# A gathered first group in every trip, and the PSUM copy behind it, in a four-layer graph network on one core

## Chip, cores and metric

The kernel runs on one core of one Trainium2 chip. The metric is the device time of one execution in microseconds (us), as the median of several runs. Below, PE is TensorE, ACT is ScalarE, DVE is VectorE, POOL is GpSimd and SP is SyncE, which here only issues DMAs.

## What is computed

Four graph networks follow each other on 3125 nodes with 64 features and 53125 edges that are sorted by target node; after each one, x = layernorm(x + network(x)).

```python
# networks 0 and 1: GIN (64-64-64 with batch norm, then 64-256-256-64)
h = x + segment_sum(x[src], dst)
# network 2: three rounds of messages, each with a GRU cell behind it
m = relu(concat(h[src], h[dst], edge_features) @ W1 + b1) @ W2 + b2
agg = segment_sum(m, dst)
# network 3: two attention layers
e = leaky_relu(alpha_s[src] + alpha_d[dst]); w = exp(e - segment_max(e)[dst])
out = segment_sum(w / (segment_sum(w)[dst] + 1e-16) * (x @ W)[src], dst) + b
```

So there are seven passes over all edges: two of GIN (passes 0 and 1), three of messages (2 to 4) and two of attention (5 and 6). Every pass fetches one row of a node table for each edge.

## The kernel before

**Edges, trips and groups.** Partition p holds 416 consecutive edges, so a "column" is 128 edges, one per partition. Eight columns are a group, four groups (j = 0 to 3) a trip, and a pass has 13 trips (0 to 12), 52 groups. DVE walks the columns of a group one after the other (`running`, L1219, and in attention L1322): a column is added to the one before wherever both edges have the same target, so the last edge of a node ends with the node's sum. SP then stores the group (`store_sums`).

**Two ways to fetch a row.** Of the 32 columns of a trip POOL gathers 20 with one indirect DMA each (`gather_group`, L794), into `ringG`, a ring of eight group slots. The other 12 columns are "fetched" by PE: the table is split into three bf16 parts side by side (128 x 192 for each of 25 blocks of 128 nodes), and a one-hot matrix of block by column picks the rows, 25 x 12 matmuls a trip (L1759), accumulated over the 25 blocks in six PSUM banks, two columns a bank. These 12 columns are the `Hot` pattern: `Hot((3, 3, 3, 3))` fetches the last three columns of each group, and the last trip of a pass `Hot((0, 0, 3, 3))`, so 26 are gathered there and 6 fetched. One trip's matmuls are called a unit here.

**A unit on PE** (`fetch_piece`). It has four pieces of 7, 6, 6 and 6 blocks. Piece 0 opens the banks one after the other, each with a matmul of `opener` (so the trace shows six such rows at the start of a unit), and the opening of a bank waits until ACT has copied the unit before out of that bank (semaphore `evicted`). The last piece closes the banks one after the other (`bank_done`). The banks are not doubled. In the message passes PE also multiplies the edge features of one group after each piece (L1780).

**ACT** does three things in one instruction stream, written out in `act_pass`: `evict` copies the banks of a unit to SBUF (L880), `make_lent` builds one-hot tiles from the node numbers (L913, one ACTIVATE of 128 x 1536 a block), and a group's own work: `clip` is the relu of a message group (L922), `weigh` the exponentials and scalings of an attention group. In pass 0 ACT makes three blocks a piece and DVE the others; in pass 1 ACT makes four blocks in piece 0 and three in each other piece; in passes 2 to 4 one a piece, and the rest is read back from DRAM (`feed_piece` on SP); in the attention passes all is read back. `make_lent(k, i + 2, q)` writes over the tiles that unit i + 1 reads, so it waits until PE has used piece q of unit i + 1 (`hot_used`), and for the last piece until all banks of unit i + 1 are closed (`bank_done`).

**The order on ACT in trip i**: the group's own work for j = 0, `make_lent(i + 2, 0)`, the same for j = 1 and j = 2; at j = 3 first `evict(i + 1)` and then `make_lent(i + 2, 3)`. In message passes four banks are copied before the relu of group j = 3 and two behind it.

**DVE** adds the three parts of the fetched columns and puts them into the ring (`take_products`, L1201 and L1210), before the first group of the trip that has fetched columns: before j = 0, in the last trip before j = 2. POOL gathers a group eight places ahead once its slot is stored, and once the group seven places back is summed.

**SP** issues in program order: reloads of tiles, the node numbers of the fetched columns (`load_sources`), features, stores. Ahead of an attention pass it stores the node table (`tab`) and two values a node (`adtab`) in seven chunks; POOL waits for all of `adtab`, gathers one row of it, and starts the pass.

Of the kernel before, what the change touches and what calls it, by code (L numbers as in the profile page):

```python
# [18 lines left out]
COLS, GROUPS = 8, 4  # L19
# [5 lines left out]
TRIPS = L // SPAN  # L25
# [147 lines left out]
class Pass:  # L173
# [24 lines left out]
    def by_vector(self, q):  # L198
# [3 lines left out]

TILES = [range(0, 7), range(7, 13), range(13, 19), range(19, NT)]
UMAX = 12
HOT, LAST = Hot((3, 3, 3, 3)), Hot((0, 0, 3, 3))
MIXED = 64 + 3 * EF
KEPT = 3
KEEPING = 2
SOURCED = 5
STEP, TOP, PEAK = 4194304.0, 1024.0, 32.0  # L210
PASSES = ([Pass(0, HOT, LAST), Pass(1, HOT, LAST)] + [Pass(2 + l, HOT, LAST) for l in range(NLAYER)]
          + [Pass(5 + l, HOT, LAST, WG) for l in range(2)])
# [12 lines left out]
EIGHTH = L * EF // 8  # L225
COUNT_FROM, COUNT_TRIPS = 4, 6
WEIGHT_TRIPS = 8
EARLY_BANKS = 4
FIRST_AT = 9


# [35 lines left out]
def build(nc, a, out):  # L267
    with ExitStack() as ctx:  # L268
# [153 lines left out]
        def fed_tiles(way, q):  # L422

            size = UMAX * P
            return eighths(way.fed(q).start * size, len(way.fed(q)) * size).bitcast(I16)
# [159 lines left out]
        def _(sp):  # L585
# [56 lines left out]
            def trip(k, i, l=None, after_first=None):  # L642
                if k < SOURCED:
                    if i == 0 and k:
                        load_sources(k, 2)
                for j in range(GROUPS):
                    g = i * GROUPS + j
                    if k < SOURCED and i + 3 < TRIPS and j == (l is not None):
                        load_sources(k, i + 3)
                    if l is not None:  # L650
                        if g + ERING < NG:
                            load_edges(l, g + ERING)
                        if g + QRING - 1 < NG and g:
                            load_starts(l, g + QRING - 1)
                    if k and i + 2 < TRIPS:
                        feed_piece(k, i + 2, j)
                        if l is not None and j == GROUPS - 1:
                            load_hot_edges(l, i + 2)
                    store_sums(k, g)
                    if after_first is not None and j == 0:  # L660
                        after_first()

            def feed_piece(k, i, q):

                way, m = PASSES[k], k * TRIPS + i
                if i == 0:
                    sp.wait_ge(bank_done, BANKS_BEFORE[k])
                elif q < len(TILES) - 1:
                    sp.wait_ge(hot_used, (len(TILES) - 1) * (m - 1) + q + 1)
                else:  # L670
                    sp.wait_ge(bank_done, BANKS_BEFORE[k] + i * way.banks)
                sp.dma_start(fed_tiles(way, q), kept[q][i * P:(i + 1) * P, (way.fed(q).start - TILES[q].start) * UMAX * P // 2:
                                                                 (way.fed(q).stop - TILES[q].start) * UMAX * P // 2]
                             ).then_inc(hot_fed[q], 16)
# [88 lines left out]
            for l in range(2):  # L763
                if l:
                    feed_unit(5 + l, 0)
                for c in range(NC):
                    sp.wait_ge(*done(f"gh{l}", c))
                    sp.dma_start(chunk_of(tab[5 + l], c), chunk(gN, c, WG)).then_inc(table_out, 16)
                    sp.dma_start(chunk_of(adtab[l], c), chunk(adN, c, 2)).then_inc(adtab_out, 16)
                    if l == 0 and c == NC - 4:  # L770
                        sp.wait_ge(*FILL("agg2", NC - 1))
                        feed_piece(5, 0, 0)
                    if l == 0 and c == NC - 2:
                        sp.wait_ge(*FILL("l2_back", NC - 1))
                        for q in range(1, len(TILES)):
                            feed_piece(5, 0, q)
                sp.wait_ge(ad_scattered, 16 * NT * (l + 1))
                sp.dma_start(ad_e[:].rearrange("p l o -> p (l o)"), ad_g).then_inc(ad_in, 16)
                feed_unit(5 + l, 1)
                for i in range(TRIPS):  # L780
                    trip(5 + l, i)
# [83 lines left out]
        def _(act):  # L865
            def evict(k, i, banks=None):

                way, m, unit = PASSES[k], k * TRIPS + i, PASSES[k].unit(i)
                banks = range(unit.banks) if banks is None else banks
                if m and banks.start == 0:  # L870
                    act.wait_ge(parts_used, m)
                if i == 0 and 2 <= k < 5 and banks.start == 0:
                    act.wait_ge(q_scattered, 16 * NT * (k - 1))
                    act.wait_ge(qtable_out, 16 * NC * (k - 1))
                    act.wait_ge(table_out, 16 * NC * k)
                size = 3 * way.fetched
                for b in banks:
                    n = min(2, unit.u - 2 * b)
                    act.wait_ge(bank_done, BANKS_BEFORE[k] + i * way.banks + b + 1)
                    nc.scalar.copy(parts_of(way)[:, 2 * b:2 * b + n].rearrange("p u k d -> p u (k d)"),  # L880
                                   ps[:, b, 0:2 * size].rearrange("p (u x) -> p u x", u=2)[:, 0:n]
                                   ).then_inc(evicted, 1)
# [9 lines left out]
            def make_lent(k, i, q):  # L892

                way, m = PASSES[k], k * TRIPS + i
                if k < KEEPING and (i or q):
                    keep_piece(k, i - (q == 0), (q - 1) % len(TILES))
                if q == 0:
                    act.wait_ge(src_hot_in[m % 2], 16 * (m // 2 + 1))
                if k < KEEPING and i:
                    act.wait_ge(hot_kept[q], 16 * (k * TRIPS + i))  # L900
                if i == 0:
                    if q == 0 and k == 0:
                        act.wait_ge(numbered, 1)
                    elif q == 0:
                        act.wait_ge(bank_done, BANKS_BEFORE[k])
                        if k >= 2:
                            act.wait_ge(*done(f"pq{k - 2}", NC - 1))
                elif q < len(TILES) - 1:
                    act.wait_ge(hot_used, (len(TILES) - 1) * (m - 1) + q + 1)
                else:  # L910
                    act.wait_ge(bank_done, BANKS_BEFORE[k] + i * way.banks)
                for t in way.by_scalar(q):
                    ins = nc.scalar.activation(needed(way, hot_of(way)[t]), needed(way, src_hot[m % 2]),  # L913
                                               ACT.Abs_reciprocal_sqrt, bias=node_minus[:, t:t + 1], scale=STEP, saturate=False)
                ins.then_inc(lent_ready, 1)
# [18 lines left out]
                                         ).then_inc(weighted, 1)  # L934

            def act_pass(k):
                lent, banks = k < SOURCED, PASSES[k].banks
                if lent:
                    for q in range(len(TILES)):
                        make_lent(k, 0, q)  # L940
                    for q in range(len(TILES) - 1):
                        make_lent(k, 1, q)
                evict(k, 0)
                if lent:
                    make_lent(k, 1, len(TILES) - 1)
                for i in range(TRIPS):
                    for j in range(GROUPS):
                        g = i * GROUPS + j
                        if k == 0:
                            zero_starts(g)  # L950
                        elif 2 <= k < 5:
                            if j == GROUPS - 1 and i + 1 < TRIPS - bool(PASSES[k].last.first):
                                evict(k, i + 1, range(EARLY_BANKS))
                            clip(k - 2, g)
                        elif k >= 5:
                            weigh(k - 5, g)
                        if PASSES[k].last.first and i >= TRIPS - 2:
                            if i == TRIPS - 1 and j == PASSES[k].last.first - 1:
                                evict(k, i)
                        elif j == GROUPS - 1 and i + 1 < TRIPS:  # L960
                            evict(k, i + 1, range(EARLY_BANKS if 2 <= k < 5 else 0, banks))
                        if lent and i + 2 < TRIPS:
                            make_lent(k, i + 2, j)
                if k < KEEPING:
                    keep_piece(k, TRIPS - 1, len(TILES) - 1)
# [966 lines left out]
```

## Time and profile before

| | |
|---|---|
| runs, median (lowest, highest) | 3032.32 us (3028.57, 3034.46) |
| profiled execution, its own time | 3030.97 us |
| its span, first to last instruction | 3029.1 us |
| PE busy | 2631.4 us (87%) |
| POOL busy | 2187.9 us (72%) |
| DVE busy | 1936.0 us (64%) |
| ACT busy | 1495.0 us (49%) |
| mean granted TensorE clock | 0.911 of full speed |

The profile is of one execution. A row of a timeline gives start and length of equal neighbouring instructions in us, engine, line, operation, what is written and read, shape, count, and in brackets the idle time of the engine before them with what ended it. A busy PE is modelled from its starts. The granted clock is the share of full speed that PE was given; its two levels are 2.4 GHz (1.00) and 1.2 GHz (0.50). POOL's pause of 0.30 us between two gathers stands as "issue" and is part of a gather's price.

### The profile page before, as it was taken

What the parts mean: (1) busy time and instruction counts of PE and PEld (TensorE: products, weight loads), DVE (VectorE), ACT (ScalarE), POOL (GpSimd) and SP (SyncE); (2) the same over time, 40 slices, a digit from 0 to 9 for tenths busy, and PEclk for the clock granted to TensorE, in tenths of its full rate; (3) what the DMA queues carried; (4) which work ended last, traced back from release to release, by engine and by line L of the source; (5) the groups of instructions that cost most, each with busy time, mean ns of one, the idle gap of its engine ahead of it and who ended that gap; (6) DMA issues with size and microseconds to landing.
All of it is one profiled execution on the core that took longest, in us unless ns stands there. A gap on an engine that the chain in (4) does not pass through costs nothing. (4 is left out here: it accounts for less than half of the span.)

```text
span 3029.1 us, 73919 instructions
## 1 busy us (share of the span) xinstructions
PE 2631.4 (87%) x28348; PEld 2440.9 (81%) x28348; DVE 1936.0 (64%) x6197; ACT 1495.0 (49%) x2632; POOL 2187.9 (72%) x2178
## 2 busy tenths in 40 slices
PE   7999669999699999489997599994899995799981
PEld 7999649999469999279997299994499994699981
DVE  5877743554348888468888568886445555455555
ACT  7877438888234444244443344441634443344443
POOL 6777737777657777677777677776567776777774
PEclk9999859999799999699998799997799997799995
DMA  5666728998348998269997289994287775487761
GB/s 175 219 215 218 202 67 285 359 364 301 118 138 291 302 304 289 82 205 304 305 304 241 86 279 304 303 305 145 39 249 257 257 255 179 110 260 254 260 220 43
DMA packets 321465, 688.68 MB, mean 227 GB/s; under 512 B 114939, under 2 KB 150245, under 8 KB 302708
## 3 DMA queue, kind: packets, MB, share of 16 engines
q1 hardware_dynamic: 227584, 537.99, 52.8%
q0 software_dynamic: 69344, 70.04, 10.2%
q10 hardware_dynamic: 24340, 78.40, 6.6%
q8 instruction: 78, 1.28, 0.2%
q14 instruction: 119, 0.97, 0.1%
HBM read 487.50 MB, written 198.70 MB: 227 GB/s over the span
## 5 line engine op out<-in xcount | busy, mean ns | idle before, releaser
L1759 PE MATMUL ps<-big 128*128 128x192 bf16 (+1 forms) x25275 | 2260.8, 248 | 1.8 <-issue 1.7
L1759 PEld LDWEIGHTS ps<-big 128*128 128x128 fp8e4 (+1 forms) x25275 | 2136.1, 98 | 45.0 <-issue 5.7
L794 POOL DMA_INDIRECT ringG<-tab,src_i x1596 | 1600.5, 1003 | 522.1 <-issue 479.7
L1219 DVE SCALAR_TENSOR_TENSOR ringG<-ringG,same 128x64 f32<-128x64 f32 x2075 | 588.9, 284 | 126.6 <-ACT ringG L922 65.2
L913 ACT ACTIVATE big<-src_hot,node_minus 128x1536 fp8e4<-128x1536 int16 x242 | 368.9, 1573 | 189.7 <-PE ps L1759 171.5
L913 ACT ACTIVATE big<-big,node_minus 128x1536 fp8e4<-128x1536 int16 x239 | 364.4, 1573 | 174.4 <-PE ps L1759 165.9
L1219 DVE SCALAR_TENSOR_TENSOR edge_side<-edge_side,same 128x64 f32<-128x64 f32 x1245 | 347.1, 279 | 17.2
L794 POOL DMA_INDIRECT ringG<-in_x,src_i x266 | 280.9, 1056 | 92.7 <-issue 78.1
L1322 DVE SCALAR_TENSOR_TENSOR ringG<-ringG,expo 128x65 f32<-128x65 f32 x830 | 238.8, 288 | 157.0 <-ACT ringG L933 78.7
L880 ACT COPY big<-ps 128x384 f32<-128x384 f32 (+1 forms) x450 | 208.2, 481 | 191.5 <-PE ps L1759 188.0
L922 ACT ACTIVATE ringG<-ringG 128x512 f32<-128x512 f32 x156 | 98.4, 631 | 361.7 <-DVE ringG L1273 361.5
L1201 DVE TENSOR_TENSOR big<-big 128x768 f32<-128x768 f32 (+3 forms) x78 | 72.9, 935 | 294.0 <-ACT big L880 266.6
L1759 PE MATMUL ps<-opener,big 128*128 128x384 bf16 (+1 forms) x525 | 174.6, 333 | 42.9 <-DVE big L1177 18.8
L933 ACT ACTIVATE ringG<-ringG,expo 128x65 f32<-128x65 f32 x832 | 210.5, 335 | 0.0
L794 POOL DMA_INDIRECT nodes<-sums,end_i x125 | 119.3, 954 | 77.7 <-issue 62.1
L927 ACT ACTIVATE expo<-pair 128x16 f32<-128x16 f32 x104 | 22.4, 216 | 284.3 <-DVE pair L1313 284.3
L1273 DVE TENSOR_TENSOR ringG<-ringG,edge_side 128x512 f32<-128x512 f32 x156 | 108.0, 692 | 16.1
L1780 PE MATMUL ps<-w_e_mix,edge_side 128*128 128x64 bf16 x798 | 49.6, 196 | 78.4 <-DVE ringG L1269 69.4
L798 POOL DMA_INDIRECT q_at_start<-big,start_i x75 | 78.8, 1050 | 46.4 <-DVE xN L1361 23.0
L1780 PEld LDWEIGHTS ps<-w_e_mix,edge_side 128*128 128x128 bf16 x798 | 41.8, 99 | 82.3 <-issue 72.6
L968 ACT ACTIVATE big<-ps 64x512 f32<-64x512 f32 (+2 forms) x70 | 37.8, 544 | 139.7 <-PE ps L1677 75.0
L1269 DVE TENSOR_TENSOR ringG<-ringG,ps 128x320 f32<-128x320 f32 (+1 forms) x156 | 76.6, 491 | 44.9 <-DMA ringG<-tab,src_i 40.6
(269 smaller groups left out, 1731.3 us busy)
## 6 DMA issues: line engine op xcount, KB each, us to landing
big<-kept SPq DMA_DIRECT2D x117, 1152.0 KB
big<-kept SPq DMA_DIRECT2D x78, 960.0 KB
sums<-ringG SPq DMA_DIRECT2D x260, 256.0 KB
kept<-big ACTq DMA_DIRECT2D x91, 576.0 KB, 3.8
edge_side<-q_at_start SPq DMA_DIRECT2D x156, 256.0 KB
big<-kept SPq DMA_DIRECT2D x26, 1344.0 KB
big<-kept SPq DMA_DIRECT2D x52, 576.0 KB
big<-kept SPq DMA_DIRECT2D x39, 768.0 KB
```

What stands on the lines that cost most here:

```text
L794: return pool.indirect_dma_start(out=out_ap, out_offset=None, in_=table, in_offset=bass.IndirectOffsetOnAxis(ap=index, axis=0))
L798: return pool.indirect_dma_start(out=table, out_offset=bass.IndirectOffsetOnAxis(ap=index, axis=0), in_=in_ap, in_offset=None, bounds_chec ...
L880: nc.scalar.copy(parts_of(way)[:, 2 * b:2 * b + n].rearrange("p u k d -> p u (k d)"), ps[:, b, 0:2 * size].rearrange("p (u x) -> p u x", u ...
L913: ins = nc.scalar.activation(needed(way, hot_of(way)[t]), needed(way, src_hot[m % 2]), ACT.Abs_reciprocal_sqrt, bias=node_minus[:, t:t + 1 ...
L922: nc.scalar.activation(rows_of(2 + l, g), rows_of(2 + l, g), ACT.Relu).then_inc(clipped, 1)
L933: nc.scalar.activation(rows[:, u, 1:WG], rows[:, u, 1:WG], ACT.Copy, scale=expo[:, g % 2, 1, u:u + 1]).then_inc(weighted, 1)
L1219: return v.scalar_tensor_tensor(now, before if u == 0 else source[:, (u - 1) * D:u * D], same[:, c:c + 1], now, ALU.mult, ALU.add)
L1269: v.tensor_tensor(rows[:, 0:n], rows[:, 0:n], ps[:, EBANK + g % 2, 0:n], ALU.add).then_inc(edge_added, 1)
L1273: v.tensor_tensor(rows, rows, q, ALU.add).then_inc(edge_summed, 1)
L1322: ins = v.scalar_tensor_tensor(rows[:, u, 1:WG], before, expo[:, g % 2, 0, u:u + 1], rows[:, u, 1:WG], ALU.mult, ALU.add)
L1759: mm = pe.matmul(ps[:, b, 0:2 * n] if wide else ps[:, b, to:to + n], hot[t][0:rows, u * P:(u + 1) * P], opener[:, 0:2 * n] if wide else sp ...
L1780: mm = pe.matmul(ps[:, EBANK + bank, u * D:(u + 1) * D], ringE[:, s, u * P:(u + 1) * P], w_e_mix[:, l * D:(l + 1) * D], start=True, stop=True)
```

## The change

The fetched columns of a trip move to its last three groups, four each; the first group is gathered whole. A trip still has 20 gathered and 12 fetched columns and six banks, and the last trip 26 and 6. `Hot.first`, the first group with fetched columns, thereby goes from 0 to 1, and DVE's `take_products` moves behind the first group of the trip by itself. The copy of the banks moves on ACT from the last group of the trip before to the first group of the trip, behind the group's own work. On SP a load moves one group later in message passes, and two tile reloads ahead of pass 5 move behind the last table store.

```diff
-HOT, LAST = Hot((3, 3, 3, 3)), Hot((0, 0, 3, 3))
+HOT, LAST = Hot((0, 4, 4, 4)), Hot((0, 0, 2, 4))
...
-                    if k < SOURCED and i + 3 < TRIPS and j == (l is not None):
+                    if k < SOURCED and i + 3 < TRIPS and j == 2 * (l is not None):
                         load_sources(k, i + 3)
...
                     if l == 0 and c == NC - 2:
                         sp.wait_ge(*FILL("l2_back", NC - 1))
-                        for q in range(1, len(TILES)):
-                            feed_piece(5, 0, q)
+                        feed_piece(5, 0, 1)
+                if l == 0:
+                    for q in range(2, len(TILES)):
+                        feed_piece(5, 0, q)
...
-                evict(k, 0)
-                if lent:
-                    make_lent(k, 1, len(TILES) - 1)
                 for i in range(TRIPS):
                     for j in range(GROUPS):
                         g = i * GROUPS + j
                         if k == 0:
                             zero_starts(g)
                         elif 2 <= k < 5:
-                            if j == GROUPS - 1 and i + 1 < TRIPS - bool(PASSES[k].last.first):
-                                evict(k, i + 1, range(EARLY_BANKS))
                             clip(k - 2, g)
                         elif k >= 5:
                             weigh(k - 5, g)
-                        if PASSES[k].last.first and i >= TRIPS - 2:
-                            if i == TRIPS - 1 and j == PASSES[k].last.first - 1:
-                                evict(k, i)
-                        elif j == GROUPS - 1 and i + 1 < TRIPS:
-                            evict(k, i + 1, range(EARLY_BANKS if 2 <= k < 5 else 0, banks))
+                        if j == PASSES[k].unit(i).first - 1:
+                            evict(k, i)
+                            if lent and i == 0:
+                                make_lent(k, 1, len(TILES) - 1)
                         if lent and i + 2 < TRIPS:
                             make_lent(k, i + 2, j)
```

Three places in the instruction order show what moves. The first is ACT in pass 1, from the piece 2 tiles of one unit to the piece 0 tiles of the next (L913, now L914: the tiles; L880, now L881: the bank copies; L889, now L890: a store of tiles; in square brackets the semaphores waited for). Before:

```order
L913 ACTIVATE big<-big,node_minus 128x1536 [waits hot_used,hot_kept2]
L913 ACTIVATE big<-big,node_minus 128x1536 x2
L880 COPY big<-ps 128x384 [waits bank_done,parts_used]
L880 COPY big<-ps 128x384 [waits bank_done] x5
L889 DMA kept<-big 128x2304 [waits lent_ready]
L913 ACTIVATE big<-big,node_minus 128x1536 [waits bank_done,hot_kept3]
L913 ACTIVATE big<-big,node_minus 128x1536 x2
```

The same stretch with the change:

```order
L914 ACTIVATE big<-big,node_minus 128x1536 [waits hot_used,hot_kept2]
L914 ACTIVATE big<-big,node_minus 128x1536 x2
L890 DMA kept<-big 128x2304 [waits lent_ready]
L914 ACTIVATE big<-big,node_minus 128x1536 [waits bank_done,hot_kept3]
L914 ACTIVATE big<-big,node_minus 128x1536 x2
L881 COPY big<-ps 128x384 [waits bank_done,parts_used]
L881 COPY big<-ps 128x384 [waits bank_done] x5
```

The six copies stood ahead of the three ACTIVATEs that wait for the closed banks, and stand behind them now.

The second place is ACT in a message pass, from the piece 2 tile on (L922, now L923, is the relu of a group). Before:

```order
L913 ACTIVATE big<-src_hot,node_minus 128x1536 [waits hot_used]
L880 COPY big<-ps 128x384 [waits bank_done,parts_used]
L880 COPY big<-ps 128x384 [waits bank_done] x3
L922 ACTIVATE ringG<-ringG 128x512 [waits edge_summed]
L880 COPY big<-ps 128x384 [waits bank_done] x2
L913 ACTIVATE big<-src_hot,node_minus 128x1536 [waits bank_done]
L922 ACTIVATE ringG<-ringG 128x512 [waits edge_summed]
```

With the change:

```order
L914 ACTIVATE big<-src_hot,node_minus 128x1536 [waits hot_used]
L923 ACTIVATE ringG<-ringG 128x512 [waits edge_summed]
L914 ACTIVATE big<-src_hot,node_minus 128x1536 [waits bank_done]
L923 ACTIVATE ringG<-ringG 128x512 [waits edge_summed]
L881 COPY big<-ps 128x384 [waits bank_done,parts_used]
L881 COPY big<-ps 128x384 [waits bank_done] x5
```

The copies have moved behind the piece 3 tile and behind the relu of the next trip's first group.

The third place is SP ahead of pass 5 (L672, now L671: tile reloads; L768 and L769, now L767 and L768: the stores of `tab` and `adtab`; L778, now L779: a load that waits for POOL's scatters). Before:

```order
L672 DMA big<-kept 128x4608 [waits bank_done,filled]
L672 DMA big<-kept 128x4608 [waits bank_done] x2
L768 DMA tab<-nodes 128x66 [waits done_a]
L769 DMA adtab<-adN 128x2
L778 DMA ad_e<-ad_at_start 128x832 [waits ad_scattered]
```

With the change:

```order
L671 DMA big<-kept 128x4608 [waits bank_done,filled]
L767 DMA tab<-nodes 128x66 [waits done_a]
L768 DMA adtab<-adN 128x2
L671 DMA big<-kept 128x4608 [waits bank_done] x2
L779 DMA ad_e<-ad_at_start 128x832 [waits ad_scattered]
```

Two of the three reloads have moved behind the last table stores.

## Rows read from the trace of the kernel before

**Rows 1.** Windows by pass (1 and 2), POOL's gathers only; busy, clock, DMA share, GB/s.
```profile
449.00:796.00 347.00, 262.42 (x266) 0.96 0.88 310
890.80:1247.00 356.20, 275.25 (x266) 0.96 0.84 274
```
**Rows 2.** Timeline of PE, pass 1: the first openers of two units.
```profile
560.83 0.33 PE L1759 MATMUL ps<-opener,big 128*128 128x384 bf16 x1
...
586.06 0.33 PE L1759 MATMUL ps<-opener,big 128*128 128x384 bf16 x1
```
**Rows 3.** Timeline of ACT, pass 1, around the end of the same unit.
```profile
584.79 1.98 ACT L880 COPY big<-ps 128x384 f32<-128x384 f32 x5
...
587.01 4.54 ACT L913 ACTIVATE big<-src_hot,node_minus 128x1536 fp8e4<-128x1536 int16 x3
```
**Rows 4.** Timeline of PE, the first matmul behind pass 1.
```profile
799.97 1.33 PE L1668 MATMUL ps<-ringG,spans 128*128 128x64 f32 x5 [24.52 <-DVE ringG L1219]
```
**Rows 5.** Timeline of DVE, the last group of pass 1.
```profile
797.38 2.53 DVE L1219 SCALAR_TENSOR_TENSOR ringG<-ringG,same 128x64 f32<-128x64 f32 x8 [3.73 <-DMA ringG<-tab,src_i]
```
**Rows 6.** Timeline of DVE, pass 0: behind unit 11, and the first instruction behind the pass.
```profile
346.84 0.62 DVE L1177 TENSOR_SCALAR big<-src_hot,node_f 128x1536 bf16<-128x1536 int16 x1 [1.94 <-PE ps L1759]
...
383.03 0.28 DVE L1517 TENSOR_TENSOR b_pq<-b_pq,ps 128x128 f32<-128x128 f32 x1
```
**Rows 7.** Timeline of ACT, pass 2: a tile of piece 0, and a relu.
```profile
998.25 1.58 ACT L913 ACTIVATE big<-big,node_minus 128x1536 fp8e4<-128x1536 int16 x1 [1.15 <-PE ps L1759]
...
1014.85 0.63 ACT L922 ACTIVATE ringG<-ringG 128x512 f32<-128x512 f32 x1
```
**Rows 8.** Timeline of PE, pass 2: first openers of two units and of the last unit.
```profile
990.57 0.33 PE L1759 MATMUL ps<-opener,big 128*128 128x384 bf16 x1
...
1016.41 0.33 PE L1759 MATMUL ps<-opener,big 128*128 128x384 bf16 x1
...
1197.24 0.33 PE L1759 MATMUL ps<-opener,big 128*128 128x384 bf16 x1
```
**Rows 9.** Timeline of DVE, pass 2: parts added, two groups' first additions, first instruction behind the pass.
```profile
992.53 0.96 DVE L1201 TENSOR_TENSOR big<-big 128x768 f32<-128x768 f32 x1
...
995.17 0.47 DVE L1269 TENSOR_TENSOR ringG<-ringG,ps 128x320 f32<-128x320 f32 x1
...
1000.40 0.49 DVE L1269 TENSOR_TENSOR ringG<-ringG,ps 128x320 f32<-128x320 f32 x1
...
1248.62 0.49 DVE L1269 TENSOR_TENSOR ringG<-ringG,ps 128x320 f32<-128x320 f32 x1 [1.04 <-DMA ringG<-tab,src_i]
...
1253.09 0.19 DVE L1560 COPY nodes<-deg 128x25 f32<-128x25 f32 x1
```
**Rows 10.** Timeline of PE: pauses of three lengths, and matmuls at both clocks.
```profile
313.77 0.37 PE L1830 MATMUL ps<-ident,flag 128*1 128x128 f32 x1 [4.31 <-DVE edge_row L1460]
...
315.29 2.28 PE L1759 MATMUL ps<-big 128*128 128x192 bf16 x13
...
319.76 1.24 PE L1759 MATMUL ps<-big 128*128 128x192 bf16 x13
...
485.14 0.32 PE L1759 MATMUL ps<-opener,big 128*128 128x384 bf16 x1 [3.28 <-ACT big L880]
...
1212.85 0.39 PE L1780 MATMUL ps<-w_e_mix,edge_side 128*128 128x64 bf16 x8 [1.92 <-DVE ringG L1269]
```
**Rows 11.** Windows behind those pauses; busy PE, PEld, DVE, ACT, POOL, then the granted clock.
```profile
313.00:316.40 3.40, 2.01 (x10) 1.42 (x11) 2.56 (x11) 0.72 (x1) 2.48 (x4) 0.50 0.78 260
...
486.50:490.00 3.50, 3.50 (x43) 3.33 (x41) 2.73 (x5) 3.50 (x5) 2.89 (x3) 1.00 0.42 144
...
1213.50:1217.00 3.50, 3.50 (x26) 3.32 (x24) 3.32 (x16) 0.63 (x1) 2.68 (x3) 0.53 0.63 184
```
**Rows 12.** Timelines of SP and of POOL ahead of pass 5.
```profile
2194.62 2.85 SPq L672 DMA_DIRECT2D big<-kept  x3
...
2216.09 0.99 POOL L794 DMA_INDIRECT ad_row<-adtab,dst_first  x1 [12.46 <-DMA adtab<-adN]
```

More of the change, by code:

```diff
@@ L227 @@
 WEIGHT_TRIPS = 8
-EARLY_BANKS = 4
 FIRST_AT = 9
@@ L936, in act_pass @@
             def act_pass(k):
-                lent, banks = k < SOURCED, PASSES[k].banks
+                lent = k < SOURCED
                 if lent:
```

## The prediction

> **What bounds the kernel now.** I read the windows by pass first, then PE and ACT at the border of two units, then the ends of the passes, and last the granted clock behind pauses of PE. The windows [rows 1] show a pass that lasts as long as its gathers: 266 of them in 347.0 us, 1.30 us each with the 0.30 us pause, and 1.34 us each in pass 2. Taking durations and pauses (266 x 0.30 = 79.8) off, POOL waited 347.0 - 262.4 - 79.8 = 4.8 us in pass 1 and 1.2 us in pass 2. PE is the close second. In pass 1 it opens a unit every 25.23 us [rows 2], against 20 gathers at 1.30 = 26.1 us a trip, and it can because ACT's copies run in the shadow of the closing banks: five copies from 584.79, the next unit opened at 586.06 [rows 2, 3]. Through the last trip, with 26 gathers for half a unit, PE is idle 24.52 us before the pass ends [rows 4]. That idle time is the room that a slower PE may use up before it shows.
>
> **Part 1, passes 0 and 1: the copies behind the last tiles.** The order of ACT shows that the copies of unit i + 1 now stand behind `make_lent(i + 2, 3)`, which waits until all banks of unit i + 1 are closed. PE meanwhile waits at the next opener for the first of these copies. Each border thus gets a chain that nothing covers: three ACTIVATEs, 4.54 us [rows 3], one copy of about 0.5 and 0.1 of handover: 5.1 us. The piece 3 tiles made early gain nothing, since PE wants them only after 19 of a unit's 25 blocks. The first border of a pass is spared, as `evict(0)` still stands ahead.
>
> Pass 1 has 11 such borders: 11 x 5.1 = 56.1 us. Its last unit, done at 799.97 - 24.52 = 775.45 [rows 4], is then done at 831.6. What follows is the copy (0.5), half a trip's additions (about 1.2, half of the two additions of [rows 9] and a handover) and two groups at 2.6 [rows 5], ending at 838.5 instead of 800.0: **+38.5**. The gathers keep up, as POOL needs only the sums of seven groups back.
>
> Pass 0 has nine borders before unit 11: +45.9. The border behind unit 10 is free, because PE pauses there anyway for DVE (4.31 us and more, [rows 10]). DVE works without a stop from the end of unit 11, 346.84, to the end of the pass, 383.03 [rows 6], so the shift comes out whole and the border behind unit 11 hides in it: **+45.9**.
>
> **Part 2, message passes.** Here the chain is one ACTIVATE of 1.58, then the relu of the next trip's first group, 0.63 [rows 7], then a copy: 2.7 us a border, if that relu is due. It is: its group needs the edge product that PE multiplies after piece 2, and DVE reaches it some 26 us after the unit opened. On the way each relu also queues behind a tile that waits for PE's piece (the first starts 7.7 us after the opener, [rows 7, 8]), which holds DVE to PE's pace but not below it. So a unit takes 25.84 [rows 8] + 2.7 = 28.5 us, above the 26.8 of 20 gathers, and 11 borders make 29.7. The last unit of pass 2 opens at 1197.24 + 29.7 = 1226.9. From there DVE needs 2.4 for the rest of its group (an estimate from the eight sums of [rows 5]), 2.6 for parts and mixed tile, five groups at 5.23, about 1.2 for the last additions, a group of 5.2, and 4.5 for the last one [rows 9]: 42.1 us, 1269.0 instead of 1253.1. That is +16, and with three passes of the same build **+48**.
>
> **Part 3, attention passes.** No tiles are made there, so the copy follows the group's own work, which is done well before the banks close; once gathers lag, PE may lose a few us and still has over 20 us of room in its last trip. I cost this at nothing. Ahead of pass 5 POOL waits 12.46 us for `adtab`, whose last store queues behind three reloads [rows 12]; with two of them behind it I take two thirds of the wait, a little less for other traffic: **-7** (bounds 0 and -12.5). The reloads that come later land before PE's third piece.
>
> **Part 4, what else moves.** Additions, copies, gathers and stores keep their number and size; the last trip gets one small addition and three small DMAs more. SP's load of node numbers comes a group later and is used a trip later. POOL's few us of waiting [rows 1] get no credit, as PE sets the pace of those passes now.
>
> **Part 5, the clock.** The rows show three pauses: after 4.31 us PE ran at 0.50 of its clock, 13 matmuls taking 2.28 instead of 1.24 us; two such batches ran like that, so 2.1 us were lost; after 3.28 us it stayed at 1.00; after 1.92 us, in a stretch thin of matmuls, it fell to 0.53 [rows 10, 11]. The pauses of 5.1 us are longer than the one that dropped the clock, so I take 2.1 for each of the 20: **+42** (bounds 0 and 42). Those of 2.7 lie between a case without and cases with a drop: 0.8 for each of the 33, **+26** (bounds 0 and 69). The Trainium skill, "TensorE: Matmul & The Clock Gate", section "A second HAM failure mode: psum-queue depth-cycling", reports a kernel whose short pauses between groups of matmuls that take turns in PSUM banks sent the clock up and down again and again. By that rule every border here would pay; the pause of 3.28 us at 485.14 speaks against it, that of 1.92 us for it.
>
> **Sum.** 45.9 + 38.5 + 48 - 7 = 125 without the clock, 193 with it. Against the profiled execution's own 3030.97 us that is **3224 us**; that execution lies 1.4 us below the median of the runs, which changes nothing here.
>
> **Rivals.**
> - *Every border drops the clock*: 53 x 2.1 = 111 in place of 68, 3267 us. For it: the pause of 1.92 us. Against it: that of 3.28 us. The rule of the Trainium skill in part 5 gives the same.
> - *No border drops it*: 3031 + 125 = 3156 us. For it: the pauses stand in dense work, as the one of 3.28 us did. Against it: 4.31 us sufficed.
> - *Message passes stay with the gathers*: the 2.7 us shrink because the relu is not due or PE catches up. Without part 2 and its clock it is 3224 - 48 - 26 = 3150 us. For it: POOL needs 26.8 us a trip, only 1.7 less. Against it: the order of ACT is fixed.
> - *Faster*: the gathers still set the end of every pass and PE's pause disappears in its room. In pass 1 that room is 24.5 less the 6.9 of copy, additions and two groups, 17.6 us, so it decides at 1.6 us a border. Then the gain of pass 5 at its bound and POOL's waiting of pass 1 remain, 3031 - 12.5 - 4.8 = 3014 us. It would take tiles made before the banks close, which the wait in the order excludes, or copies ahead of them.
> - *Nothing moves*: the order shows that it does.
>
> **How the numbers follow.** The forecast has 0.54, every border dropping 0.15, no drop 0.14, message passes hidden 0.12, faster 0.04, nothing 0.01. The range, 3140 to 3275, takes in the first four, less what may lie beyond their own errors; about 0.15 to 0.2 is left out. A measurement of this kernel can tell about 0.2% (6 us) from no change; all but the last two rivals lie far above it, so slower has 0.95, faster 0.04, the same 0.01.
>
> **What would show it.** In the profile after: in passes 0 and 1, an idle time of PE of about 5 us ahead of each first opener, ended by ACT's copy, and units about 30 to 32.5 us apart; on ACT three ACTIVATEs right behind the closing of the banks and the copies behind them. In message passes a pause near 2.7 us and 28.5 to 30 us a unit, POOL waiting for DVE's sums in passes 0 to 4, passes 5 and 6 still ended by gathers, and POOL's wait for `adtab` cut to 4 to 6 us. The granted clock should dip behind the long pauses. I am wrong if PE's units in pass 1 stay near 25 us apart, or if the passes still end one group behind POOL's last gather.

## The result, and the profile after

The changed kernel takes 3246.26 us (median of 4 runs, 3240.59 to 3249.38) against 3033.39 us before, measured beside it: a ratio of 1.070 (95% interval 1.067 to 1.072), some 213 us more. The profiled execution took 3249.38 us, its span is 3247.6 us. The forecast was 3224 us, with a range of 3140 to 3275.

The page of the changed kernel; first the busy times and the chain that ended last, then the group of the opening matmuls.

```profile
PE 2718.5 (84%) x28348; PEld 2505.7 (77%) x28348; DVE 1936.3 (60%) x6206; ACT 1469.6 (45%) x2632; POOL 2156.7 (66%) x2178
...
PE 73%; ACT 8%; issue 7%; DVE 6%; POOL 5%; DMA 1%; SPq 0%; ACTq 0%; POOLq 0%; DVEq 0%
...
L1754 PE MATMUL ps<-opener,big 128*128 128x384 bf16 (+1 forms) x525 | 192.0, 366 | 247.0 <-ACT big L881 158.2
```

The same group before:

```profile
L1759 PE MATMUL ps<-opener,big 128*128 128x384 bf16 (+1 forms) x525 | 174.6, 333 | 42.9 <-DVE big L1177 18.8
```

DVE has the work that it had. PE issues the same 28348 matmuls and is busy for 2718.5 instead of 2631.4 us, and ahead of the openers it stands idle for 247.0 instead of 42.9 us, most of it ended by ACT's bank copy. Longer pauses and slower matmuls are the two things to look for. The timeline of ACT at a border in pass 1, which answers to [rows 3]:

```profile
583.28 4.50 ACT L914 ACTIVATE big<-big,node_minus 128x1536 fp8e4<-128x1536 int16 x3 [1.43 <-PE ps L1754]
587.69 0.46 ACT L881 COPY big<-ps 128x384 f32<-128x384 f32 x1
...
588.04 1.99 ACT L881 COPY big<-ps 128x384 f32<-128x384 f32 x5
```

And PE at the same border:

```profile
588.29 0.48 PE L1754 MATMUL ps<-opener,big 128*128 128x384 bf16 x1 [5.11 <-ACT big L881]
588.56 2.29 PE L1754 MATMUL ps<-big 128*128 128x192 bf16 x13
590.64 0.53 PE L1754 MATMUL ps<-opener,big 128*128 128x384 bf16 x1
590.96 1.47 PE L1754 MATMUL ps<-big 128*128 128x192 bf16 x13
592.26 0.33 PE L1754 MATMUL ps<-opener,big 128*128 128x384 bf16 x1
592.42 1.24 PE L1754 MATMUL ps<-big 128*128 128x192 bf16 x13
```

The three tiles wait for the banks to close at 583.28 and only then is the first bank copied, so PE opens 5.11 us late. Then 13 matmuls take 2.29 us, the next 13 still 1.47, before they are back at 1.24. A border of a message pass, ACT and PE:

```profile
1133.73 1.58 ACT L914 ACTIVATE big<-src_hot,node_minus 128x1536 fp8e4<-128x1536 int16 x1 [4.10 <-PE ps L1754]
1135.21 0.61 ACT L923 ACTIVATE ringG<-ringG 128x512 f32<-128x512 f32 x1
1135.73 1.60 ACT L881 COPY big<-ps 128x384 f32<-128x384 f32 x4
```

```profile
1077.65 0.32 PE L1754 MATMUL ps<-opener,big 128*128 128x384 bf16 x1 [2.52 <-ACT big L881]
1077.81 1.23 PE L1754 MATMUL ps<-big 128*128 128x192 bf16 x13
...
1106.16 0.32 PE L1754 MATMUL ps<-opener,big 128*128 128x384 bf16 x1 [2.52 <-ACT big L881]
1106.33 1.79 PE L1754 MATMUL ps<-big 128*128 128x192 bf16 x13
```

One tile, the relu, then the copies: a pause of 2.52 us, behind which the matmuls sometimes run at full speed (1077.81) and sometimes slow down within the first batch (1106.33).

The windows of passes 1 and 2 on POOL's gathers, which answer to [rows 1] (length, busy time and count, granted clock, DMA share, GB/s):

```profile
518.90:927.60 408.70, 261.42 (x266) 0.92 0.79 260
1027.20:1392.70 365.50, 266.39 (x266) 0.96 0.81 264
```

The gathers are as long as before in pass 1 and shorter in pass 2 (266.4 against 275.3 us), but now POOL waits: 408.7 - 261.4 - 79.8 = 67.5 us in pass 1. The gathers no longer set the pace.

The profiled times by pass, from PE's first opener (pass 0: from the start of the span) to the end of DVE's last sum, worked out from the timelines of the kernel before, the changed one and the experiments below, in us:

| | before | after | e1 | e2 | e3 | e4 | e5 | e6 | e7 | e8 |
|---|---|---|---|---|---|---|---|---|---|---|
| pass 0 | 383.1 | 452.4 | 383.4 | 452.0 | 384.1 | 449.6 | 385.4 | 383.3 | 449.4 | 383.9 |
| pass 1 | 346.1 | 412.9 | 350.4 | 414.7 | 347.8 | 390.6 | 350.2 | 353.0 | 403.6 | 348.6 |
| pass 2 | 366.7 | 392.3 | 358.9 | 389.3 | 370.6 | 393.1 | 367.7 | 358.0 | 396.2 | 354.9 |
| pass 3 | 366.7 | 395.5 | 358.5 | 386.5 | 370.2 | 392.6 | 368.3 | 358.2 | 392.8 | 354.4 |
| pass 4 | 369.8 | 398.6 | 365.3 | 386.5 | 370.7 | 398.9 | 369.2 | 364.4 | 398.2 | 358.3 |
| last sum of pass 4 to first gather of pass 5 | 102.0 | 98.6 | 96.4 | 101.3 | 95.7 | 96.3 | 97.4 | 92.2 | 97.8 | 101.6 |

Pass 0 costs 69.3 us more, pass 1 66.7, the message passes 83.2 together, and 3.4 us come back ahead of pass 5. That is 215.8 of the 218.4 us between the two profiled executions. How far one execution can differ from another shows in e5, which changes nothing ahead of pass 5: its passes 0 and 1 are some 2 and 4 us longer than before, its message passes within 2 us.

### The profile page after: what moved, and what is told of

Read it like the earlier page. It is cut to its first block, busy times and chain, and to the rows that moved or that the text cites. A ratio compares the mean times of both kernels' runs of the same rounds, so it can differ in the third digit from the quotient of the medians.

```text
span 3247.6 us, 73931 instructions
## 1 busy us (share of the span) xinstructions
PE 2718.5 (84%) x28348; PEld 2505.7 (77%) x28348; DVE 1936.3 (60%) x6206; ACT 1469.6 (45%) x2632; POOL 2156.7 (66%) x2178
## 4 chain that ended last, share of the span: by engine, by line
PE 73%; ACT 8%; issue 7%; DVE 6%; POOL 5%; DMA 1%; SPq 0%; ACTq 0%; POOLq 0%; DVEq 0%
PE ps L1754 65%; ACT big L914 4%; PE ps L1706 4%; POOL ringG L795 2%; DVE ringG L1214 2%; POOL nodes L795 1%; PE ps L1715 1%; ACT big L963 1%; POOL ad_at_start L799 1%; DVE edge_side L1214 1%; ACT ringG L923 1%; ACT big L881 1%; ACT ringG L934 1%; DMA ringG<-tab,src_i 1%; PE ps L1672 1%
## 5 line engine op out<-in xcount | busy, mean ns | idle before, releaser
L1754 PE MATMUL ps<-big 128*128 128x192 bf16 (+1 forms) x25275 | 2328.6, 252 | 1.9 <-issue 1.9
L1754 PEld LDWEIGHTS ps<-big 128*128 128x128 fp8e4 (+1 forms) x25275 | 2192.8, 100 | 61.8 <-issue 21.2
L795 POOL DMA_INDIRECT ringG<-tab,src_i x1596 | 1575.8, 987 | 640.9 <-issue 461.2
L914 ACT ACTIVATE big<-src_hot,node_minus 128x1536 fp8e4<-128x1536 int16 x242 | 368.6, 1568 | 471.0 <-PE ps L1754 453.0
L914 ACT ACTIVATE big<-big,node_minus 128x1536 fp8e4<-128x1536 int16 x239 | 364.1, 1568 | 459.7 <-PE ps L1754 454.3
L1754 PE MATMUL ps<-opener,big 128*128 128x384 bf16 (+1 forms) x525 | 192.0, 366 | 247.0 <-ACT big L881 158.2
L795 POOL DMA_INDIRECT ringG<-in_x,src_i x266 | 274.0, 1030 | 169.3 <-DVE ringG L1214 88.2
L1754 PEld LDWEIGHTS ps<-opener,big 128*128 128x128 fp8e4 (+1 forms) x525 | 55.4, 105 | 257.6 <-issue 256.8
L881 ACT COPY big<-ps 128x384 f32<-128x384 f32 (+1 forms) x450 | 188.9, 487 | 74.1 <-PE ps L1754 73.8
L923 ACT ACTIVATE ringG<-ringG 128x512 f32<-128x512 f32 x156 | 96.0, 615 | 103.6 <-DVE ringG L1268 103.6
L1172 DVE TENSOR_SCALAR big<-src_hot,node_f 128x1536 bf16<-128x1536 int16 x91 | 56.6, 633 | 72.2 <-PE ps L1754 72.2
L1172 DVE TENSOR_SCALAR big<-big,node_f 128x1536 bf16<-128x1536 int16 x78 | 48.4, 630 | 73.9 <-PE ps L1754 73.9
```

Of the source, the lines that this page charges most:

```text
L795: return pool.indirect_dma_start(out=out_ap, out_offset=None, in_=table, in_offset=bass.IndirectOffsetOnAxis(ap=index, axis=0))
L923: nc.scalar.activation(rows_of(2 + l, g), rows_of(2 + l, g), ACT.Relu).then_inc(clipped, 1)
L1172: ins = v.tensor_scalar(hot_of(way)[t], src_hot[i % 2], node_f[:, t:t + 1], 1.0 / PEAK, ALU.is_equal, ALU.mult)
L1754: mm = pe.matmul(ps[:, b, 0:2 * n] if wide else ps[:, b, to:to + n], hot[t][0:rows, u * P:(u + 1) * P], opener[:, 0:2 * n] if wide else sp ...
```

## Experiments

Theory: the whole loss comes from the bank copies that stand behind the tiles of the last piece on ACT, by PE's pauses and by the clock that falls in them. Rival: the new pattern of columns, or SP's moves, carry part of it.

**e1, the copies ahead of the tiles again, all else as changed.** In message passes four banks are copied ahead of the relu of group j = 3 and two behind it, as before. `act_pass` is that of the kernel before again; the edit to it, in short:

```diff
+if j == GROUPS - 1 and i + 1 < TRIPS:
+    evict(k, i + 1)
-if j == PASSES[k].unit(i).first - 1:
-    evict(k, i)
 make_lent(k, i + 2, j)
```

> The changed kernel with the order on ACT as before (the copies of a unit's banks ahead of the tiles of the last piece), the new pattern of columns and SP's moves kept. Theory (the copies that wait behind the last tiles cost the whole of it): PE's pause at a border of pass 1 falls from 5.1 us to under 1 us, a unit of pass 1 comes every 25 to 26.5 us, the granted clock rises from 0.895 to 0.905 or more, and the time is 3020 to 3045 us. Rival (the pattern carries part of the loss: groups with four fetched columns, sums that come late, SP's loads a group later): over 3100 us, with pauses at the borders that another wait ends.

Measured: 3011.92 us, ratio to before 0.993 (0.9914 to 0.9947). The border of pass 1, where nothing is idle:

```profile
587.92 0.33 PE L1761 MATMUL ps<-opener,big 128*128 128x384 bf16 x1
588.08 1.24 PE L1761 MATMUL ps<-big 128*128 128x192 bf16 x13
```

The order on ACT carries the loss: mending it takes 234 us off the changed kernel. It came out below the expected 3020 us, so the rest of the change is worth some 20 us once the order is right, and e1 beats both kernels. The table says where: 7.9, 8.2 and 4.5 us in the message passes and 5.7 us ahead of pass 5, less 4.3 us in pass 1, which is about what the profiled execution of e5 differs by there.

**e2, only the copies moved behind the last tiles, pattern and SP as before.**

```diff
-                            if j == GROUPS - 1 and i + 1 < TRIPS - bool(PASSES[k].last.first):
-                                evict(k, i + 1, range(EARLY_BANKS))
                             clip(k - 2, g)
...
-                        elif j == GROUPS - 1 and i + 1 < TRIPS:
-                            evict(k, i + 1, range(EARLY_BANKS if 2 <= k < 5 else 0, banks))
+                        elif j == GROUPS - 1 and i + 1 < TRIPS and not lent:
+                            evict(k, i + 1)
                         if lent and i + 2 < TRIPS:
                             make_lent(k, i + 2, j)
+                        if lent and j == GROUPS - 1 and i + 1 < TRIPS - bool(PASSES[k].last.first):
+                            evict(k, i + 1)
```

> The kernel before, its pattern and SP's order kept, with only the copies moved on ACT behind the tiles of the last piece (still ahead of the next trip's first group). Theory: passes 0 and 1 get the same chain of three tiles and a copy, a pause of 5.1 us at each border and some 65 us each; in message passes the chain is one tile and a copy, 2.2 us, and some 20 to 30 us each, and the sums are wanted by the first group at once; together 3200 to 3260 us. Rival (the order of ACT is harmless, the pattern costs): 3025 to 3060 us.

Measured: 3222.24 us, ratio 1.063 (1.061 to 1.065). Passes 0 and 1 lose what they lose in the changed kernel, with the same pause:

```profile
586.34 0.48 PE L1759 MATMUL ps<-opener,big 128*128 128x384 bf16 x1 [5.11 <-ACT big L880]
```

The message passes, where the relu is not in the chain, pause for 2.0 us a border and lose 22.6, 19.9 and 16.6 us, the last two just below the 20 to 30 expected. So the order alone costs 191 us, with neither the pattern nor SP's moves.

**e3, the copies where the change puts them, the last tiles behind them.**

```diff
 evict(k, i)
-if lent and i == 0:
-    make_lent(k, 1, len(TILES) - 1)
-if lent and i + 2 < TRIPS:
+if lent and i + 1 < TRIPS:
+    make_lent(k, i + 1, len(TILES) - 1)
+if lent and i + 2 < TRIPS and j < GROUPS - 1:
     make_lent(k, i + 2, j)
```

> The changed kernel with the copies where the change puts them (behind the first group of a trip), but with the tiles of the last piece moved behind these copies. Theory (not the place of the copies costs, but the tiles ahead of them): PE's pauses in pass 1 under 1 us; in message passes at most the relu of the first group, 0.6 us; 3020 to 3060 us. Rival (a copy behind a group's own work is late by itself): pauses stay at 2 us or more in the message passes, 3080 us or more.

Measured: 3037.75 us, ratio 1.0018 (1.0008 to 1.0027). Pass 1 has no pause; the message passes keep one, relu and copy, longer than the 0.6 us expected, and no unit behind it was slower than without a pause:

```profile
1052.46 0.32 PE L1754 MATMUL ps<-opener,big 128*128 128x384 bf16 x1 [1.36 <-ACT big L881]
```

The place of the copies behind the first group's own work is thus the small part of the loss: the message passes are 11.7, 11.7 and 5.4 us longer than in e1, and the kernel as a whole takes 26 us more, of the 234. The tiles ahead of the copies make the rest, 208 us.

**e4, PE kept busy through the pauses of pass 1.**

```diff
 settle()
+if k == 1 and q == 0 and not first:
+    for _ in range(48):
+        pe.matmul(ps[:, 7, 0:192], opener[:, 0:P], opener[:, 0:192], start=True, stop=True)
```

> The changed kernel with 48 matmuls of 128x192 more at each border of pass 1 alone, into a bank that nobody reads; they take up PE's pause of 5.1 us (48 x 0.095 = 4.6 us at full clock) and change nothing else. Theory (each pause drops the clock and the matmuls behind it run at half speed): the pause of 0.5 us leaves the granted clock of pass 1 at 0.98 or more, its units come 30.6 us apart instead of 32.5, and the time is 16 to 24 us less than the changed kernel's, about 3226 us. Rival (units are longer for another reason, tiles or transfers that come late): no difference, within 5 us of 3246. Rival (the added matmuls themselves hold PE up): 3250 us or more.

Measured: 3223.76 us, 22.5 less than the changed kernel, and pass 1 is 22.3 us shorter.

```profile
577.01 4.12 PE L1744 MATMUL ps<-opener 128*128 128x192 bf16 x48
582.28 0.32 PE L1757 MATMUL ps<-opener,big 128*128 128x384 bf16 x1 [1.15 <-ACT big L881]
582.44 1.23 PE L1757 MATMUL ps<-big 128*128 128x192 bf16 x13
```

The windows of pass 1, of the changed kernel and of e4 (length; busy PE, PEld, DVE, ACT, POOL; granted clock, DMA share, GB/s):

```profile
523.70:936.60 412.90, 342.48 (x3750) 329.21 (x3750) 169.30 (x480) 275.86 (x240) 257.59 (x263) 0.91 0.78 256
```

```profile
520.40:911.00 390.60, 366.36 (x4326) 358.52 (x4326) 169.57 (x480) 275.87 (x240) 257.89 (x263) 0.98 0.83 271
```

The wait is the same, ACT's copy ends it as before; only the useless matmuls are new, and the kernel is faster for them. The clock's share of pass 1 is shown by itself: 22.3 of 66.7 us, 2.0 a border.

**e7, half of that filling (24 matmuls).**

> As e4_busy_pause, with 24 matmuls instead of 48: PE's pause at a border of pass 1 is then 2.8 us. In the other runs pauses of 1.1 and 1.4 us never lowered the clock, those of 2.0 in a few cases, those of 2.5 in a third to a half, those of 4.8 and 5.1 always. Theory (the length of the pause decides): some of the borders drop, the gain against the changed kernel lies between 6 and 20 us, 3226 to 3240 us. Rival (any filling keeps the clock, since the rest of the pause is shorter than that of 3.28 us that kept it in the kernel before): all 11 borders keep it, 3224 us. Rival (the half of the filling is wasted): all drop, 3246 us.

Measured in one run: 3239.10 us; pass 1 is 9.3 us shorter than in the changed kernel. Three borders:

```profile
582.05 0.48 PE L1757 MATMUL ps<-opener,big 128*128 128x384 bf16 x1 [3.13 <-ACT big L881]
582.32 2.28 PE L1757 MATMUL ps<-big 128*128 128x192 bf16 x13
...
615.35 0.48 PE L1757 MATMUL ps<-opener,big 128*128 128x384 bf16 x1 [3.13 <-ACT big L881]
615.63 2.28 PE L1757 MATMUL ps<-big 128*128 128x192 bf16 x13
...
647.41 0.32 PE L1757 MATMUL ps<-opener,big 128*128 128x384 bf16 x1 [3.13 <-ACT big L881]
647.57 1.23 PE L1757 MATMUL ps<-big 128*128 128x192 bf16 x13
```

The same pause of 3.13 us dropped the clock at six of the eleven borders and left it alone at five. Neither rival holds.

**e5, the kernel before with only SP's move ahead of pass 5:** the reloads of pieces 2 and 3 behind the loop of the table stores.

```diff
-    for q in range(1, len(TILES)):
-        feed_piece(5, 0, q)
+    feed_piece(5, 0, 1)
+if l == 0:
+    for q in range(2, len(TILES)):
+        feed_piece(5, 0, q)
```

> The kernel before with only SP's move ahead of pass 5 (the reloads of pieces 2 and 3 behind the last table store). The prediction's term was -7 us, with POOL's wait for adtab cut from 12.46 to 4 to 6 us. Theory now (the reloads share the DMA engines with the last stores, so moving two of them right behind helps little): the wait falls to 7 to 10 us and the time by 2.5 to 5.5 us, 3026 to 3029 us. Rival (the predicted term was right): 7 us or more, 3024 us or less. Rival (nothing): 3031 us.

Measured: 3029.55 us beside 3033.51, ratio 0.9985 (0.9976 to 0.9994). POOL's wait here, and in the changed kernel, against 12.46 us in [rows 12]:

```profile
2225.50 0.99 POOL L796 DMA_INDIRECT ad_row<-adtab,dst_first  x1 [7.91 <-DMA adtab<-adN]
```

```profile
2433.18 0.99 POOL L795 DMA_INDIRECT ad_row<-adtab,dst_first  x1 [9.89 <-DMA adtab<-adN]
```

A gain of 4.0 us by the medians and 2 to 7 by the interval, a little over half of the predicted term.

**e6, e1 with the reloads of pieces 1 to 3 held until the last store has landed.**

```diff
-        feed_piece(5, 0, 1)
 if l == 0:
-    for q in range(2, len(TILES)):
+    sp.wait_ge(adtab_out, 16 * NC)
+    for q in range(1, len(TILES)):
         feed_piece(5, 0, q)
```

> The kernel with the new pattern and the copies ahead of the last tiles (e1_copies_first, 3011.9 us), and the reloads of pieces 1 to 3 ahead of pass 5 held until the last adtab store has landed. Theory (reloads in flight hold the landing of adtab up, and PE, which gets its tiles later, has room in pass 5): POOL's wait falls from 7.15 us to 2 to 4 us, the time to 3007 to 3010 us. Rival (the small stores land late by themselves): the wait stays at 6 to 7 us and the time at 3010 to 3014 us. Rival (the room of PE in pass 5 is too small): over 3016 us.

```profile
2195.16 1.07 POOL L796 DMA_INDIRECT ad_row<-adtab,dst_first  x1 [2.69 <-DMA adtab<-adN]
```

Measured: 3010.45 us, ratio to before 0.9929 (0.9916 to 0.9943). The wait falls from 7.15 to 2.69 us as expected, so the reloads do hold the landing up. Which of them does is not separated: e6 takes piece 1 from ahead of the last store as well as pieces 2 and 3 from behind it. The packets in the traces speak for piece 1. A reload is 128 packets of 9216 bytes. When the last packet of `adtab` moved, all 384 of the three reloads had been moved in the kernel before, 141 in e1, little more than one reload, and none in e6. From that packet to POOL's start another 4.1 us went by in e1 and 1.9 in e6, but also 3.8 before, where none of the three was left; so what pieces 2 and 3 cost behind the store stays open. The time is 1.5 us below e1, within what these runs can tell, and just above the 3007 to 3010 expected.

**e8, the kernel before with DVE's second addition cut to 64 columns.** 448 of the 512 columns of q are left out of the message sums. The run asks why e1's message passes are shorter than before.

```diff
-v.tensor_tensor(rows, rows, q, ALU.add)
+v.tensor_tensor(rows[:, 0:D], rows[:, 0:D], q[:, 0:D], ALU.add)
```

> The kernel before with DVE's second addition of a message group (rows + q, 128x512) cut to its first 64 columns; 448 of 512 columns of q are left out of the sums. In the kernel before 46 of 52 gathers of pass 2 that met this addition took 1.14 to 1.39 instead of 0.94 us, 12.5 us a pass, and in e1_copies_first 9, at 2.7 us. Theory (the addition holds POOL's gathers up, and the gain of 8 us a message pass in e1 comes from where it falls): POOL's gathers of pass 2 sum to 262 to 266 instead of 275.3 us, and each message pass is 6 to 11 us shorter, 2998 to 3013 us. Rival (e1's gain comes from the pattern's later need of the fetched columns): gathers get shorter, but the passes by under 3 us each, 3022 us or more.

Measured: 3000.43 us, ratio 0.990 (0.9886 to 0.9917); the gathers of pass 2 sum to 261.4 us, and the message passes are 11.5 to 12.2 us shorter each, somewhat more than expected. DVE has less to do in this run, but that is not what shortens the passes: in pass 2 the stretch from the first gather to the last is 14.0 us shorter, and 13.8 of that is time of the gathers themselves. What happens is seen in pass 2 of the kernel before, POOL and then DVE:

```profile
984.78 0.94 POOL L794 DMA_INDIRECT ringG<-tab,src_i  x1 [0.30 <-issue]
986.03 1.14 POOL L794 DMA_INDIRECT ringG<-tab,src_i  x1 [0.30 <-issue]
```

```profile
985.67 0.69 DVE L1273 TENSOR_TENSOR ringG<-ringG,edge_side 128x512 f32<-128x512 f32 x1
```

And in e1:

```profile
985.11 0.94 POOL L796 DMA_INDIRECT ringG<-tab,src_i  x1 [0.30 <-issue]
986.35 0.94 POOL L796 DMA_INDIRECT ringG<-tab,src_i  x1 [0.30 <-issue]
```

```profile
985.70 0.69 DVE L1275 TENSOR_TENSOR ringG<-ringG,edge_side 128x512 f32<-128x512 f32 x1
```

Before, a gather starts while the addition runs, and takes 1.14 us. In e1 the addition falls into the middle of a gather and both are undisturbed. With the two timelines laid side by side, 46 gathers over 1.0 us in pass 2 before have this addition as their main overlap on DVE, together 12.5 us over the 0.94 of an undisturbed one; in e1 it is 9, at 2.7 us. So the addition holds the gathers up (shown), and e1 gains by where it falls (read from the trace; no run moved the addition alone).

## Why the prediction was right, point by point

**The chain on ACT (parts 1 and 2): right.** Three tiles and a copy make a pause of 5.1 us in pass 1, as costed. In message passes the units open 29.42 us apart in pass 2 against 25.83 before (mean of eleven). The pause and the overlap of an opener with its forerunner make 2.7 of that, the forecast's border; the rest is the clock. From the last opener to DVE's last sum pass 2 takes 42.5 us, costed at 42.1. e2 shows that this order costs 191 us by itself, and e1 that without it nothing of the loss is left.

**Pass 1, +38.5 and 23 of clock forecast, +66.7 measured.** e4 gives the clock's 22.3, close to the 23 in part by luck: 2.7 of it fall to the unit behind the first border, which the forecast had spared and where a pause of 4.6 us dropped the clock. The other 5 us lie in small things: without the clock a border cost 5.27 us rather than 5.1 (e4's units open 30.50 us apart, those before 25.23), since the overlap of an opener with its forerunner is lost too, and from PE's last matmul to DVE's last sum 9.6 us went by where 6.9 were costed.

**Pass 0, +45.9 and 19 forecast, +69.3 measured.** The nine pauses came, 5.1 us early and 4.8 us late in the pass, and with the overlaps they make 45.7. The units behind them were 1.4 to 2.6 us longer, 21.0 together, for which the step had 19 from [rows 10]. The border behind unit 11 was to hide in DVE's work and did not: from the end of unit 11 to the end of the pass it took 40.8 instead of 36.3 us. Unit 11 itself was 2.7 us shorter, which gives part of that back.

**Message passes, +48 and 26 forecast, +83.2 measured: the clock term was too small.** The +48 was right. A unit is 27.5 us long where the clock fell and 25.9 where it did not, 1.65 apart; that happened to 21 of the 33 units 1 to 11, 35 us instead of 26, and leaves 48 of the 83.2. The step took 0.8 us for each border, between a row with a drop and rows without; the measured mean is 1.05.

**Ahead of pass 5, -7 forecast: mis-sized.** The step took two thirds of the wait, on the reading that the store queues behind the reloads. The wait was 9.89 us instead of 4 to 6, and 7.2 to 8.1 in the five other runs with this move (e1, e3, e4, e5, e7). The packets agree with the queue: all three reloads ahead of the last packet of `adtab` before, 153 of their 384 packets in the changed kernel. But the saving is not shared out by their number: only e6, with all three held back, comes to 2.69 us. So two reloads of three were worth 2.6 us of the wait here and 4.3 to 5.3 in the other runs, not two thirds of it.

**Luck.** Little was needed. Each term came out on the same side, 4.4, 5.2, 9.2 and 3.6 us above the forecast for pass 0, pass 1, the message passes and the start of pass 5, so none of these errors hid another.

**What was costed at nothing: right.** In passes 5 and 6 PE paused 5.0 and 6.6 us at the first border, and the gathers still set the end, 337.6 and 337.2 us against 338.5 and 338.1. That POOL's waits and the pattern get no credit where PE sets the pace holds too: the shorter gathers of pass 2 (266.4 us) bought nothing in the changed kernel; they show in e1 and e6.

**The rivals.** "Every border drops the clock" falls: 10 of 30 units behind a pause in the message passes kept it. "No border drops it" falls by every border of pass 1, and "message passes hidden" by their 83 us. "Faster" named its condition, copies ahead of the tiles, and that is e1: the room is then not used up, and the time is 3011.92 us, near the 3014 given, though by another way (shorter gathers in the message passes, not POOL's waits in pass 1).

The rule of the Trainium skill in part 5 ("TensorE: Matmul & The Clock Gate", section "A second HAM failure mode: psum-queue depth-cycling"), short pauses between groups of matmuls that send the clock up and down, was seen here: eleven drops at eleven borders of pass 1. As a rule for every border it went too far for the short pauses of the message passes.

## What to carry to other kernels

On an engine that works in program order, an instruction that frees a resource (here the copy out of an undoubled PSUM bank) belongs ahead of any that waits for the same event and is needed later; ask of each wait what is queued behind it and who waits for that. A pause on TensorE can cost more than its length: a chain of 5 us at a border cost 7 in pass 1. And a change made of several parts should be measured with each part undone: here a loss of 234 us from the order on one engine hid a gain of 20 from the rest (e1).

## What the runs showed of the hardware

**Pauses and the clock.** In these passes, pauses at a border had these outcomes (units 2 to 12 of pass 1, or 2 to 11 of the three message passes, that ran slow afterwards): 1.1 us in e4, none of 11; 1.4 us in e3, none of 30; 2.0 us in e2, 10 of 30; 2.5 us in the changed kernel, 20 of 30; 3.1 us in e7, 6 of 11; 5.1 us in pass 1 of the changed kernel, all of 11. The expectation to e7 puts those of 2.5 us at a third to a half; they were two thirds. The length alone does not decide in between: three borders of 3.13 us in one pass came out differently. The outcomes are not scattered, though: in pass 2 of the changed kernel units 2, 5, 8 and 11 kept the clock and the others behind a pause lost it, and in e7 two borders that lost it and two that kept it took turns. What else decides was not tested. One drop cost 1.65 us in the message passes, and 1.4 to 2.5 us in units 2 to 11 of pass 1. Filling the pause with matmuls that nobody reads won 22.5 us.

**An addition on VectorE that delays gathers.** A 128x512 f32 addition of two SBUF operands lengthened a gather of GpSimd that began in its first 0.5 us from 0.94 to mostly 1.14 or 1.39 us, whose end came 1.51 us after the addition's start either way; one that had begun 0.6 us earlier was not delayed, and the addition took 0.69 us in both cases. The Trainium skill, "SBUF — State Buffer", section "Who interferes with whom", says that a VectorE instruction with two SBUF inputs contends with a GpSimd instruction that reads SBUF, and that the order of issue decides who blocks. The trace agrees for a gather that starts second, but does not show the reverse: where the gather came first, the addition was not lengthened. That the gather reads its indices at its start would explain both, but is an inference.
